# Batch 0's start rearranged (identity first, squares and low parts on VectorE, values last, late setup), with new order tables

## The reference

```
q = rms_norm(split_heads(x @ w_q.T)); k = rms_norm(split_heads(x @ w_k.T))
v = split_heads(x @ w_v.T)
scores = tanh(q @ k.T / sqrt(8) / 50) * 50            # causal mask behind it
y = softmax(scores) @ v;  x = layernorm(x + y @ w_o.T)
```

## Time and profile before

| | us |
|---|---|
| median of 3 runs | 832.19 |
| lowest and highest | 831.43 and 833.56 |
| the profiled execution | 831.95 |
| its span | 830.0 |
| busy PE / DVE / ACT / POOL | 678.9 / 595.4 / 554.2 / 392.0 |
| mean granted TensorE clock | 0.828 |

### The profile page before, as it was taken

The page is one execution under the profiler, slowest core; times in us unless marked ns, Lnnn a source line. Parts: engine busy times, 40 slices in busy tenths (PEclk is TensorE's granted clock), DMA queues, the critical chain, the costliest instruction groups (busy, mean ns, idle before and its releaser), DMA issues.

```text
span 830.0 us, 16995 instructions
## 1 busy us (share of the span) xinstructions
PE 678.9 (82%) x6576; PEld 401.4 (48%) x6576; DVE 595.4 (72%) x1681; ACT 554.2 (67%) x403; POOL 392.0 (47%) x399
## 2 busy tenths in 40 slices
PE   3588787889979988999899988998899879865652
PEld 2344334455546455645455545645565535434232
DVE  4442718777787788958888788769896986588455
ACT  0588688889768876959768876788687968600000
POOL 5263436447544574346455664446546543421201
PEclk8567678899789987989789987899799979985755
DMA  6321302033300503030304030120303030000001
GB/s 190 64 42 37 64 13 53 25 61 119 64 14 17 112 12 67 27 64 14 64 14 90 14 64 15 50 54 2 64 26 65 2 64 27 13 1 26 0 0 51
DMA packets 96913, 36.75 MB, mean 44 GB/s; under 512 B 68018, under 2 KB 94146, under 8 KB 96834
## 3 DMA queue, kind: packets, MB, share of 16 engines
q1 hardware_dynamic: 96834, 35.67, 18.8%
HBM read 14.69 MB, written 4.19 MB: 23 GB/s over the span
## 4 chain that ended last, share of the span: by engine, by line
PE 61%; DVE 18%; issue 10%; ACT 7%; POOL 3%; DMA 1%; POOLq 0%; DVEq 0%; ACTq 0%
PE ps_y L1199 16%; PE ps_s L1182 14%; ACT pr L731 4%; PE ps_m L1308 3%; PE ps_m L1230 3%; ACT th L716 3%; PE ps_m L1206 3%; PE ps_a L1230 3%; PE ps_m L1356 2%; PE ps_a L1393 2%; DVE v_aug L844 2%; PE ps_m L1258 2%; PE ps_a L1206 2%; PE ps_a L1258 1%; PE ps_a L1292 1%
## 5 line engine op out<-in xcount | busy, mean ns | idle before, releaser
L716 ACT ACTIVATE th<-ps_s 128x1024 f32<-128x1024 f32 (+1 forms) x256 | 280.2, 1129 | 110.7 <-PE ps_s L1182 102.0
L627 POOL TENSOR_TENSOR pr<-pr,tri 128x320 f32<-128x320 f32 (+1 forms) x256 | 194.8, 784 | 186.7 <-ACT pr L731 186.7
L731 ACT ACTIVATE pr<-th 128x2304 f32<-128x2304 f32 x128 | 271.5, 2122 | 15.5 <-PE ps_y L1199 15.4
L1182 PE MATMUL ps_s<-q_st,k_st 32*64 32x512 f16 (+7 forms) x2048 | 193.1, 319 | 24.9 <-ACT th L716 20.8
L1199 PE MATMUL ps_y<-pr,v_aug 128*32 128x512 f32 (+7 forms) x2048 | 157.4, 439 | 0.4 <-POOL pr L627 0.4
L1182 PEld LDWEIGHTS ps_s<-q_st,k_st 32*64 32x64 f16 x2048 | 92.3, 114 | 120.0 <-issue 54.3
L1199 PEld LDWEIGHTS ps_y<-pr,v_aug 128*32 128x32 f32 x2048 | 57.0, 113 | 66.9 <-issue 47.4
L641 POOL TENSOR_TENSOR st<-qk,st 128x1024 f16<-128x1024 f32 x32 | 73.8, 2327 | 32.3 <-DVE st L860 32.3
L629 POOL TENSOR_TENSOR k_wide<-qkT,head_of 128x1024 f32<-128x1024 f32 x16 | 30.1, 1902 | 58.0 <-DVE qkT L1029 58.0
L629 POOL TENSOR_TENSOR r<-x,rw_row 128x512 f32<-128x512 f32 x16 | 18.9, 1180 | 63.6 <-DVE x L922 63.6
L702 ACT ACTIVATE hq<-hu 128x512 f32<-128x512 f32 x8 | 5.0, 630 | 60.7 <-POOL hu L629 60.7
(11 more groups left out here) (220 smaller groups left out, 1133.9 us busy)
## 6 DMA issues: line engine op xcount, KB each, us to landing
x_in<-in_L_attn_x SPq DMA_DIRECT2D x16, 256.0 KB, 2.8
x_res<-in_L_attn_x SPq DMA_DIRECT2D x16, 256.0 KB, 3.1
result<-y_out SPq DMA_DIRECT2D x16, 256.0 KB, 2.4
mask_a<-in_L_ffn_attention_mask SPq DMA_DIRECT2D x3, 1024.0 KB, 5.2
pr<-in_L_ffn_attention_mask SPq DMA_DIRECT2D x2, 1024.0 KB, 8.6
w_sb<-in_L_ffn_w SPq DMA_DIRECT2D x2, 256.0 KB
q_st<-st SPq DMA_TRANSPOSE x16, 4.5
k_st<-st SPq DMA_TRANSPOSE x16, 4.7
```

What stands on the lines that cost most here:

```text
L627: return nc.gpsimd.tensor_tensor(buf, buf, tri[:, None, :].to_broadcast([P, blocks, 64]), ALU.mult)
L716: nc.scalar.activation(th[:, gi % 2, c0:c1], ps_s[:, c0:c1], ACT.Tanh, scale=1.0 / (QK_SCALE ** 2 * DH ** 0.5 * SOFTCAP))\
L731: nc.scalar.activation(pr[:, probs_at(n):probs_at(n) + GROUP], th[:, gi % 2, :], ACT.Exp, scale=SOFTCAP).then_inc(exp_done, 1)
L1182: last = mm(ps_s[64 * s:64 * s + 64, COL[kb]:COL[kb] + S - 64 * kb], k_st[rows, k, gi // 2, 64 * kb:64 * kb + 64], q_st[rows, k, gi // 2, ...
```

## The change

It has six parts.

1. POOL fills and completes `ident` first, under a semaphore of its own (`ident_ready`); PE waits for that alone. The rest of the constants are waited for by the routed setup. PE waits for the `wT` copy only ahead of batch 0's q and k.
2. For batch 0 alone, DVE squares q and k and computes the low parts; POOL's steps return at once for it.
3. Batch 0's values are copied behind the low parts, and not behind q and k. (The values get a semaphore track `val` of their own.)
4. The routed setup comes behind those values on DVE. On PE it moves behind the first group's scores. Its end, the copies of sine and cosine (`setup_trig`), comes behind batch 1's `hi`.
5. The Sin moves from the head of ACT's program to the place before the exp of the second group (n == 1).
6. The four tables, `BANK` and `BANK_READ` are new.

```diff
         def _(pool):
-            nc.gpsimd.memset(ident[:, :], 0.0).then_inc(const_ready, 1)
+            nc.gpsimd.memset(ident[:, :], 0.0).then_inc(ident_ready, 1)
+            pool.wait_ge(ident_ready, 1)
+            nc.gpsimd.affine_select(out=ident[:, :], in_=ident[:, :], compare_op=ALU.not_equal, fill=1.0, base=0,
+                                    pattern=[[-1, P]], channel_multiplier=1).then_inc(ident_ready, 1)
...
         def _(act):
-            act.wait_ge(setup_ve, SETUP_RED)
-            nc.scalar.activation(turn[:, :, :, :], red[:, :, :, :], ACT.Sin).then_inc(setup_act, 1)
-
...
+                        if n == 1:
+                            act.wait_ge(setup_ve, SETUP_RED)
+                            nc.scalar.activation(turn[:, :, :, :], red[:, :, :, :], ACT.Sin).then_inc(setup_act, 1)
...
             def prep_ss(b, k):
+                if b.no == 0:
+                    ve["prep"].wait(v, b, "qk1")
+                    pl["prep"].done(nc.vector.tensor_tensor(qk2, qk_flat, qk_flat, ALU.mult), "sq", b)
...
                 if b.no == 0:
+                    ve["prep"].wait(v, b, "hi_k")
+                    for s, part in enumerate("qk"):
+                        pl["prep"].done(nc.vector.tensor_tensor(lo_parts[s], qk_twice[s], hi_parts[s], ALU.subtract),
+                                        f"lo_{part}", b)
+                    prep_v(b, k, True)
                     setup_routed()
+                if b.no == 1:
+                    setup_trig()
...
-            t_.wait_ge(const_ready, 19)
+            t_.wait_ge(ident_ready, 2)
             t_.wait_ge(attn_weights_in, 16 * 4)
...
-            t_.wait_ge(setup_ve, 1)
...
+                        if g and g[0].no == 0 and g[2] == 0 and half == 1:
+                            setup_routed()
...
-    ["att.o@-2", "fin.res/1@-1", "att.oT@-2", "fin.ln/1@-1"], ["route.row/0@-1", "att.x1f@-2"],
...
+    ["late.root1@-3"], ["prep.hi/1@0", "att.o@-2", "fin.yT/1@-1", "route.w/0@-1", "att.oT@-2"],
+    ["fin.res/1@-1", "att.x1f@-2"], ["att.ss@-2", "fin.ln/1@-1"],
...
-    "sel.ET": ["fin.yT/0@1", "late.z1@-1"],
+    "sel.ET": ["fin.res/0@1", "late.z0@-1"],
```

More of the change, by code:

```diff
@@ L107 @@
 PE_ORDER = (
[L108 to L123, removed]
+    ["route.thr/1@-2", "att.S0@-2"], ["att.S1@-2", "pv.4/1@-1"],
@@ L124 @@
+    ["route.won/1@-1", "prep.v/0@1"], ["fin.y1T/0@0", "late.w2@-2", "sel.gather@-1"],
+    [], ["sel.gather1@-1", "fin.yT/0@0"],
+    ["late.sc0@-2", "late.sc1@-2", "fin.wo/0@0"], ["pv.0/1@0", "pv.1/1@0"],
+    ["sel.ET@-1", "pv.2/1@0"], ["sel.hnT@-1", "pv.3/1@0", "sel.qkv@-1"],
+    ["sel.R@-1", "sel.R1@-1", "sel.R2@-1"], ["sel.R3@-1", "sel.qkT@-1", "prep.xT/1@1"],
+    ["sel.RT@-1"], ["fin.y0T/1@0", "sel.msel@-1"],
 )
 VE_ORDER = (
-    ["sel.msel@-2", "fin.y0/1@-1", "att.sc0@-2"], ["att.mx0@-2", "att.sc1@-2", "att.mx1@-2"],
@@ L134 @@
[L134 to L139, removed]
@@ L140 @@
-    ["late.z0@-2", "sel.root1@-1", "sel.root2@-1", "sel.hn@-1"], ["prep.hi/0@1", "late.z1@-2"],
-    ["fin.res/0@0"], ["sel.ET@-1", "sel.hnT@-1"],
+    ["prep.xT/1@0", "sel.RT@-2", "fin.y0/1@-1", "sel.msel@-2", "att.sc0@-2"],
+    ["att.mx0@-2", "att.sc1@-2", "att.mx1@-2", "fin.x1/0@-1", "route.coef/1@-2", "prep.qk0/1@0"],
+    ["att.den@-2", "prep.qk1/1@0", "att.PT0@-2"],
+    ["fin.yU1/1@-1", "prep.v/1@0", "att.PT1@-2", "prep.ss/1@0", "prep.root1/1@0"],
+    ["fin.y1/1@-1", "prep.root2/1@0", "late.ln@-3"], ["prep.qkn/1@0"],
@@ L144 @@
 )
 POOL_ORDER = (
-    ["sel.zb@-2", "route.xw/0@-1"], [],
-    ["prep.sq/1@0"], [],
+    ["sel.zb@-2"], ["route.xw/0@-1"],
+    [], ["prep.sq/1@0"],
     [], [],
@@ L167 @@
     [], [],
-    ["att.exp@-2"], [],
+    [], ["att.exp@-2"],
     [], [],
@@ L174 @@
     [], [],
-    ["att.tanh@-2"], [],
+    [], ["att.tanh@-2"],
     [], [],
@@ L232 @@
 BANK_READ = {
-    "att.P0": ["fin.y0/1@1", "prep.qk0/1@2", "sel.qkT@0"],
+    "att.P0": ["att.sc1@0", "prep.qk1/1@2"],
     "att.P1": ["att.PT0@0"],
@@ L469, in tracks @@
         def tracks(engine, steps):
-            return {n: Track([sem(f"{engine}_{n}{k}") for k in range(2 if n in ("prep", "fin", "route") else 1)], names)
+            return {n: Track([sem(f"{engine}_{n}{k}") for k in range(2 if n in ("prep", "val", "fin", "route") else 1)], names)
                     for n, names in steps.items()}
```

143 lines of the change are left out of this document (84 added, 59 removed).

## The result

The changed kernel takes 847.12 us (median of 4 runs, 845.05 to 854.79), the kernel before, on the same chip, 831.84 (831.43 to 833.56): 1.0196 times as long, 95% interval 1.0131 to 1.0262. On another chip it took 847.20 against 833.47, 1.0191 (1.0134 to 1.0248). The forecast was 822, the range 810 to 840: the sign and the range were both wrong. Medians and ranges here are of all executions of a kernel, ratios and their intervals of the fast ones alone (within 1.5% of the fastest of the same kernel), so that the two can differ by a few tenths of a per cent.

What follows compares the result with a forecast made beforehand. No engine is full; PE comes nearest, partly at the lower clock, so its waits were taken to decide. Start 0, pairs -8.4 and end -2.0 from 831.95 gave 821.55 us, 821.8 as median; range 810 to 840.

Steps and rivals of the forecast that it cites:

- The start, up to batch 1: From the first weights to batch 1: first scores 2.4 us earlier, near 28, but batch 1's scores staying at 64.2.
- that rival: ACT's two table switches around the Sin cost 5.3 us, drain included, putting 2.4 on the forecast: 824.2; chance 0.04.
- Term of the start: 0: All that the start gains is spent when batch 1 begins: 0 us, bounds -3.0 and +1.5.
- The pairs, -8.4: Middle pairs: new order tables save 1.2 us a pair net, in seven pairs, -8.4.
- the tables do nothing: Rival for the pairs: the order tables only move waits about; 830 to 833, taken as 831.5; chance 0.13.
- The 2.3: Middle pairs: a new PE wait of 2.3 us ahead of `att.oT`, because DVE finishes `att.o` late.
- the 3.30 that were to go: Middle pairs: PE's wait of 3.30 us ahead of `hn`'s transposition was to shrink to about 0.5.
- the 1.7 us a pair: Middle pairs: gain of 1.7 us where the next pair's q and k run at full clock, 1.13 each.
- The premise under this term: Middle pairs: a wait of PE is followed by a stretch at 0.5 of the clock.
- The other shifts I count at 0: Middle pairs: moved mask products, `late.sc1` a unit behind the yT transposition and POOL's `route.xw` a group earlier cost 0.
- The slower rival: Half clock behind a longer wait before `att.oT` hits work PE is late with: +1.5 a pair, +10.5, 840.7; chance 0.25.
- The end, -2.0: End of the kernel: `sel.ET`'s shorter wait gains 1.4 us, the earlier scatter factor 0.6; -2.0, bounds 0 and -3.

Runs made afterwards that it cites:

- e1: The changed kernel with the order tables and bank assignments of the kernel before, so the new start alone: 844.53 us, 1.0147 of the kernel before.
- e4: The kernel before with q's rounding of batch 0 repeated twice on DVE, a shift of 1.4 us: 844.36 us.
- e5: The kernel before with q's rounding of batch 0 repeated four times on DVE, a shift of 2.8 us: 843.22 us.
- e10: The kernel before with q's rounding of batch 0 repeated once on DVE, a shift of 0.7 us: 840.20 us.
- e2: The kernel before with the new order tables and bank assignments, its start as before: 831.44 us, 0.9997 of the kernel before.
- e7: The kernel before with twelve unread transpositions of the identity in TensorE's 3.30 us wait ahead of `hn`'s transposition: 833.84 us, 0.9995.

## Why the prediction was wrong, point by point

**The start, up to batch 1: right, but for one point.** TensorE's first row came at 4.67 against 4.56: the identity gained nothing (0.45 forecast), because `w_o` landed at 4.54, not at 4.1. Not waiting for the `wT` copy gained 0.9 instead (x transposed at 5.69 against 6.56), the "at most 0.9" that I had counted at 0. Squares and low parts, and the DMAs behind them, as forecast:

```profile
12.05 1.22 DVE L867 TENSOR_TENSOR st<-qk 128x1024 f32<-128x1024 f32 x1
...
19.63 2.36 DVE L883 TENSOR_TENSOR st<-qk,st 128x1024 f16<-128x1024 f32 x2
...
27.85 1.00 PE L1208 MATMUL ps_s<-q_st,k_st 32*64 32x512 f16 x4 [3.31 <-DMA k_st<-st]
```

First scores at 27.85 (forecast 28), first tanh 3.1 us earlier (3.0). The Sin and its two loads on ACT, as the earlier trace rows had them:

```profile
38.61 1.28 ACT L741 ACT_TABLE_LOAD   x1
39.91 0.31 ACT L741 ACTIVATE y_out<-y_out 128x128 f32<-128x128 f32 x1
40.23 1.28 ACT L742 ACT_TABLE_LOAD   x1
41.53 2.12 ACT L742 ACTIVATE pr<-th 128x2304 f32<-128x2304 f32 x1
```

2.92 us from the first load's start to the exp. There is 0.02 between a load and the instruction behind it, and the tanh ahead of the first load ends where the load starts. So the 1380 ns of drain that the Trainium skill gives for a switch beside a load of 1283 (ScalarE: Activation LUTs, section "What ACT_TABLE_LOAD costs") are not seen here, only the load, and that rival is out. The masking took 1.53 for 2.51 and `pv.0` came at 54.32, forecast 54.5. But batch 1's first scores came at 61.83 and not at 64.2: POOL's low parts began at 53.72, 0.7 earlier, and took 4.22 instead of 4.67, and the scores also no longer waited for ACT as they did in the earlier trace rows. The second exp came 0.5 later than before, where I had 1.2. By batch 1's first exp 1.3 us of the gain were left.

**"Term of the start: 0": wrong, and this is the step that costs most.** The arithmetic up to batch 1 was nearly right; what failed is that I stopped there and took for granted that a shift at the start costs itself and no more. By e1, e4, e5 and e10 it costs the old order 6.6 to 12.5 us. In the new order the same start is the difference between 831.4 and 847.1, where I had 0 with bounds of -3.0 and +1.5. Why a shift of a microsecond moves the rows that run at the half clock stays open.

**The pairs, -8.4: wrong.** The new order alone brought 0.6 (e2), and nothing that can be measured; this was the rival "the tables do nothing", with 0.13. Even that is the end's gain: by its exps e2's profile (833.26, the slowest of its ten) loses 4.1 us between batches 1 and 14 and makes up 2.0 behind it. The waits went nearly where I said. In the pair below `hn`'s transposition waits no more, and the new wait is 1.92 us, forecast 2.3, but one item further, ahead of the product with `w_o`, for the copy `att.oT` that the router's sum holds up. TensorE in the pair from 462.7 to 552:

```profile
502.34 0.66 PE L1409 MATMUL ps_a<-wo,oT 128*128 128x128 f32 x2 [1.92 <-DVE oT L1094]
502.93 2.57 PE L1226 MATMUL ps_y<-pr,v_aug 128*32 128x384 f32 x16
...
508.57 0.33 PE L1414 MATMUL ps_a<-ident,hn 128*128 128x128 f32 x1
...
513.28 0.16 PE L1298 MATMUL ps_a<-count,ident 128*128 128x4 f16 x1 [1.72 <-issue]
...
514.84 2.08 PE L1259 MATMUL ps_m<-wT,xT 128*128 128x256 f32 x4
516.71 1.91 PE L1259 MATMUL ps_a<-wT,xT 128*128 128x256 f32 x4
```

From the values' copy to `att.o`'s end it is 12.0 us (486.39 to 498.42), where 12.2 was worked out from the earlier trace rows. So that chain was right, and yet it isn't what makes the 1.92. The last instruction of the router's sum is, on DVE:

```profile
499.90 2.10 DVE L957 TENSOR_SCALAR x<-x,rb 128x4 f32<-128x4 f32 x1
501.92 0.28 DVE L1094 COPY oT<-ps_a 128x128 f32<-128x128 f32 x1
```

It has 4 elements a partition and takes 2.10 us here, in six pairs of the changed kernel, but 0.23 at 515.00. POOL's two low parts run from 497.38 to 501.97, and the long instruction ends at 502.00, just behind them. In the kernel before it took 1.38 beside the same low parts. Without this meeting the copy would be done about 1.9 us earlier, nearly all of the wait (an estimate from these rows; no run moved the low parts). The 2.3 came near by luck: ahead of `att.oT`, where I had put it, there is no wait. I also hadn't seen the row at 513.28 in TensorE's fence: `route.won` waits 1.72 for the bank that DVE's copy of the first FFN product reads (it ends at 513.17). 1.92 and 1.72 are 3.64, no less than the 3.30 that were to go. q and k, forecast at 1.13 each, took 2.08 and 1.91; between 155 and 605 us both ran at the full clock in one pair of six (603.38: 1.13 and 1.10). By e7, too, a wait of 1.46 in place of 3.30 doesn't bring the 1.7 us a pair. The premise under this term, that a wait of TensorE is followed by a stretch at 0.5, holds for the wait of the earlier trace rows but not for every wait: behind the 1.11 us at 443.49 the kernel before stays at the full clock.

**"The other shifts I count at 0": wrong at `late.sc1`, where the new start meets it.** There its row is 18 us (847.1 to 828.9); with the old start it is nothing (831.4 to 831.6). I had looked at how far the yT transposition lies ahead of it, and not at the DVE copy between the two, nor at what stands behind the row: the scores that ACT is waiting for.

**The slower rival** came near in time, and had the wrong place. At `att.oT` the half clock does cover the `pv` half, and ACT waits 6.15 us behind it:

```profile
508.68 2.16 ACT L724 ACTIVATE th<-ps_s 128x1024 f32<-128x1024 f32 x2 [6.15 <-PE ps_s L1208]
```

But cutting that row is worth 2.1 us at most, not the 10.5 that I had put on it. Its 840.7 is near the 847 by luck.

**The end, -2.0: right.** `sel.ET` waits 0.23 where it waited 2.38, and from the scatter ahead of it to the end the changed kernel makes up 2.8 of its lag (783.90 against 766.12, then 845.0 against 830.0). The scatter factor comes 0.6 earlier after the `w2` products, as forecast (829.46 to 831.57, against 813.87 to 816.59).

In sum, by the exps: -1.3 up to batch 1 (forecast 0), +18.1 from there to batch 14 (forecast -8.4), -1.9 behind it (forecast -2.0): 14.9, of the span's 15.0.

## What to carry to other kernels

In a kernel like this one, with TensorE, DVE and ACT 82, 72 and 66% busy and a third of TensorE's time at the half clock, a change at the start can't be costed by the start alone: shift the old kernel by a microsecond first, by repeating a harmless instruction, and see what that does. Here 1.4 us cost 11.5, more than any part of the change was meant to bring. And run the two halves of a change apart as well as together: here each order with the old start took 831 to 832, the new start with the old order 844.5, and only a third edit showed what the two did to each other. In an order written out by hand, look at every row between two units that feed the engine which is waiting, and ask of each item in it what it waits for, on which bank, and what can hold that up. Moving one unit ahead of such an item was worth 18 us with the new start, nothing with the old one, and cost 5.5 in the old order: it has to be measured in the kernel that it is meant for. And a wait taken from one row is a gain only if the next row isn't waiting for the same engine.
